# A chunk of image columns turned on GpSimd instead of ScalarE

## What is computed

```python
h = tok(x)                    # patches: einsum('bsd,hd->bsh', patches, W) + b, class token, + pos
h = concat([h, txt], axis=1)
h = h + attn(layernorm(h))    # phases tanh(x @ Wk), tanh(x @ Wq); values x @ Wv; causal sums over rows; gate; @ Wo
h = h + ffn(layernorm(h))     # 64 experts, top 2 of each row, 256 slots an expert; and a shared expert
```

## Time and profile before

| | us |
|---|---|
| median of three runs (lowest, highest) | 1647.76 (1645.76, 1649.63) |
| the profiled execution, its own time | 1646.93 |
| its span, first to last instruction | 1644.2 |
| PE busy in the span | 1455.5 |
| DVE busy | 1432.7 |
| ACT busy | 1246.3 |
| POOL busy | 1012.6 |

### The profile page before, as it was taken

One profiled execution on the slowest core, in us unless ns is written; L12 is line 12 of the kernel. 1 busy time (PEld: TensorE's weight loads), 2 busy tenths in 40 slices (PEclk: granted clock), 3 DMA queues, 4 the chain that ended last, 5 costly groups with the idle time before them and its releaser, 6 DMA issues.

```text
span 1644.2 us, 30506 instructions
## 1 busy us (share of the span) xinstructions
PE 1455.5 (89%) x9030; PEld 1121.5 (68%) x9030; DVE 1432.7 (87%) x5763; ACT 1246.3 (76%) x2190; POOL 1012.6 (62%) x857
## 2 busy tenths in 40 slices
PE   2689999999999999999999999999999972776671
PEld 1467777777777777777777777777777751555551
DVE  3369999999999999999999999999999983886661
ACT  2799999999999999999999999999999741111110
POOL 0116666666666666666666666666666665788887
PEclk9899999999999999999999999999999996998885
DMA  9977777777777777777677777777776102676653
GB/s 170 245 157 151 147 145 145 141 143 133 129 124 127 123 121 120 121 123 116 120 120 120 117 117 119 119 121 121 117 119 113 39 19 65 101 117 105 94 82 34
DMA packets 257947, 195.67 MB, mean 119 GB/s; under 512 B 59000, under 2 KB 237275, under 8 KB 257784
## 3 DMA queue, kind: packets, MB, share of 16 engines
q1 hardware_dynamic: 216280, 175.30, 59.6%
q0 software_dynamic: 39296, 17.55, 8.7%
q10 hardware_dynamic: 2208, 0.89, 0.4%
HBM read 84.28 MB, written 83.73 MB: 102 GB/s over the span
## 4 chain that ended last, share of the span: by engine, by line
PE 75%; POOL 10%; issue 5%; DVE 4%; DMA 3%; ACT 3%; SPq 1%; POOLq 0%; DVEq 0%
PE bank L896 12%; POOL out_rows L640 9%; PE bank L966 8%; PE bank L949 7%; PE bank L1037 6%; PE bank L1046 5%; PE bank L920 5%; PE bank L934 4%; PE bank L904 4%; PE bank L1053 3%; PE bank L1022 2%; PE bank L985 2%; PE bank L1012 2%; PE bank L1008 2%; PE bank L1002 2%
## 5 line engine op out<-in xcount | busy, mean ns | idle before, releaser
L596 POOL DMA_INDIRECT slot_rows<-xs,slot x640 | 648.9, 1014 | 447.4 <-DVE slot L1382 278.0
L657 ACT ACTIVATE img<-img 84x980 f32<-84x980 f32 x190 | 340.5, 1793 | 13.7 <-DMA img<-in_x 7.1
L896 PE MATMUL bank<-img,w_tok 126*128 126x392 f32 (+1 forms) x640 | 228.1, 504 | 29.2 <-DMA img<-img 23.7
L640 POOL DMA_INDIRECT out_rows<-img,etok x128 | 198.7, 1552 | 54.9 <-issue 36.1
L580 POOL TENSOR_TENSOR rs<-ve,neg_half 128x12 f32<-128x12 f32 (+1 forms) x66 | 150.0, 2273 | 111.2 <-DVE ve L1265 111.2
L896 PEld LDWEIGHTS bank<-img,w_tok 126*128 126x128 f32 (+1 forms) x640 | 124.0, 195 | 115.2 <-issue 23.9
L949 PEld LDWEIGHTS bank<-pos_a,v 128*128 128x128 f32 x768 | 139.8, 190 | 42.6
L727 ACT ACTIVATE xs<-h,nb,rs 128x128 f32<-128x128 f32 x384 | 154.1, 481 | 2.5 <-DVE nb L1271 2.5
L949 PE MATMUL bank<-pos_a,v 128*128 128x325 f32 (+2 forms) x768 | 155.7, 338 | 0.0
L740 ACT ACTIVATE xh<-h,nb,rs 128x128 f32<-128x128 f32 x384 | 154.0, 480 | 0.6 <-DVE nb L1271 0.6
L966 PE MATMUL bank<-a_t,v 128*128 128x325 f32 (+2 forms) x768 | 150.3, 345 | 0.6 <-DVE a_t L1325 0.6
(11 more groups left out here) (196 smaller groups left out, 3581.6 us busy)
## 6 DMA issues: line engine op xcount, KB each, us to landing
img<-in_x SPq DMA_DIRECT2D x384, 150.1 KB
img<-img SPq DMA_DIRECT2D x254, 160.8 KB
img<-img SPq DMA_DIRECT2D x128, 128.6 KB
out_rows<-fin SPq DMA_DIRECT2D x128, 128.0 KB
slot_rows<-xs,slot POOLq DMA_INDIRECT x640
slot_rows<-init_rows SPq DMA_DIRECT2D x16, 540.0 KB, 8.9
img<-slot_rows SPq DMA_DIRECT2D x32, 270.0 KB
h<-in_txt SPq DMA_DIRECT2D x64, 128.0 KB
```

What stands on the lines that cost most here:

```text
L596: g.indirect_dma_start(out=slots_d, out_offset=bass.IndirectOffsetOnAxis(ap=slot[0:nt, q.x, part, r:r + 1], axis=0), in_=xs[0:nt, q.x, par ...
L640: g.indirect_dma_start(out=out, out_offset=bass.IndirectOffsetOnAxis(ap=etok[:, q.load, m:m + 1], axis=0), in_=ysum[:, q.load, m, :], in_o ...
L657: a.activation(cols[:, b0:b0 + nb, :], raw[:, q.u, :].rearrange("p (t b) -> p b t", b=P)[:, b0:b0 + nb, :], ACT.Copy)\
L896: ins = mm(bank[:, 5, 0:2 * PATCHES], w_tok[r, m, :], xk[r, k.u, :, m, :], start=(m == 0), stop=(m == SHIFT - 1))
```

## The change

GpSimd turns chunk 2 of each pair from pair 2 on, at the head of its `body`, ahead of the scatters of pair k-8 and of `rstd` of pair k-4. Its waits are those that ScalarE's turn had. ScalarE leaves that chunk out, except for pair 1, and turns chunks 0 and 1 as before. The order on SP, VectorE and TensorE stays the same.

```diff
--- before.py
+++ after.py
@@ -609,9 +609,20 @@
+            def turn_columns_2(q):
+
+                wait_dma(pool, s_xin, q, 2 * C)
+                wait_dma(pool, s_spread[2], q, 2, 1)
+                b0, nb = CHUNKS[2]
+                g.tensor_copy(cols[:, b0:b0 + nb, :], raw[:, q.u, :].rearrange("p (t b) -> p b t", b=P)[:, b0:b0 + nb, :])\
+                    .then_inc(S["a_d2"], 1)
+
             def body(k):
+                p2 = k.back(2)
                 p4 = k.back(4)
                 p8 = k.back(8)
+                if p2.runs():
+                    turn_columns_2(p2)
                 if p8.runs():
                     ready(p8)
                     scatter(p8, 0)
@@ -675,7 +686,7 @@
             def early(q, n):
 
-                return (q.c, n) in ((0, 2), (0, 1), (0, 0))
+                return q.c == 0 or n == 2 and q.c > 1
```

## The result

The changed kernel takes 1673.27 us in the median (1671.41 to 1678.90), the kernel before 1647.65 beside it: a ratio of 1.0161 with a 95% interval of 1.0134 to 1.0189, so 25.6 us slower. The profiled execution after took 1672.33 us around a span of 1670.5. From L615 on (behind GpSimd's new lines), a line of the kernel before has a number higher by 11 in the changed one; each experiment's lines are those of its own trace.

The account below looks back on a forecast made before the run. TensorE was taken as the bound, VectorE 0.1 us a step behind. 57 steps x 0.6 = 34.2 us later, less 3.2 while filling, gives +31.0: 1678.8 us in the median, range 1644 to 1697.

Parts of the forecast that it names:

- TensorE bound, VectorE close behind it: Even part, 20.0 us a step: TensorE has no idle time, VectorE is 0.1 us a step behind, ScalarE has room.
- its room: VectorE in the even part: only 0.1 us a step is spent waiting for another engine.
- ScalarE's chunk: 1.55 us a pair leaves ScalarE: worth nothing in the even part, 3.2 us (0 to 4.3) while the pipeline fills.
- The copy on POOL: GpSimd's turn of chunk 2 takes 1.53 us, from 721.15 to 722.7, inside its wait for `slots`; harmless for POOL.
- a fixed 18.5 us: Landing of chunk 2's spread follows the last `slots` by 18.5 us, however long the step is.
- The wait on VectorE: Small VectorE instructions before `slots` wait 0.7 us for the copy's end; less 0.1 of room, 0.6 us a step.
- the likeliest case: The forecast wait on VectorE, at 0.45 to 0.85 us a step: 1670 to 1693 us, chance 0.58.
- The signs: Expected in the trace: step 20.5 to 20.8 us, TensorE idle 0.6 of it at L1037 or L966, ScalarE's L734 wait growing.
- No wait: Rival: the copy doesn't delay VectorE, only the 3.2 us gain is left: 1644.6 us (1643 to 1648), chance 0.22.
- A short wait: Rival: VectorE and POOL take turns, a small instruction grows 0.13 to 0.28 us: about 1650 us (1647 to 1655), chance 0.14.
- Two collisions: Rival: the copy starts right behind the scatters and `score_sum` waits too, 1.1 us: 1702 us, chance 0.06.
- The two arguments for no wait: First pair's copies ran side by side on POOL and VectorE; L1285 kept 165 ns beside `rstd`'s power: a wait of 0.

Follow-up runs that it names:

- the copy added: Kernel before, ScalarE still turning all three chunks, plus a GpSimd copy of 84x784 constant values into a tensor nobody reads: 1684.5 us, ratio 1.0221.
- the memset: Kernel before, ScalarE turning all three chunks, plus GpSimd writing 84x784 zeros and reading nothing at the changed kernel's place: 1647.62 us, ratio 1.0003.
- four values: Changed kernel, but GpSimd's copy moves only 4 values a partition instead of 784, with place and waits kept: 1644.09 us, ratio 0.9982.
- two buffers: Changed kernel with two buffers for chunk 2, its turn not waiting for the last spread: 2003.11 us, ratio 0.9832, on a chip with another bound.

## Why the prediction was right

**TensorE bound, VectorE close behind it: right; its room was mis-sized.** I took 0.1 us, from the 33 waits of `h` in the earlier trace rows. That view leaves the shortest waits out. VectorE waited for TensorE at `h` in all 57 steps, and the room there was 0.21 us; another 0.1 came back because VectorE, running earlier, meets the scatters at another point. Together 0.29.

**ScalarE's chunk: 3.2 us in the fill, nothing in the even part: right; that the traces give 3.5 is partly luck.** TensorE's wait for `xh` at pair 4 went from 2.35 to 1.08 us: 0.84 us late at the token product ahead of it, TensorE is 0.64 early behind it. The 1.56 for `sl` at pair 5 is gone, and 1.4 us with it. But two more shifts stand in the traces that I had no term for, 1 us lost before 67 us and 1.4 won between 93 and 98, and most of both goes with TensorE's granted clock. It was at half in the changed kernel from 57.0 to 60.5 us, where the kernel before had the full one, and in the kernel before from 93.8 to 97.2, where the changed one had the full one. This is the product there, before and after:

```profile
94.65 3.58 PE L966 MATMUL bank<-a_t,v 128*128 128x325 f32 x12
```

```profile
92.99 0.79 PE L1033 MATMUL bank<-const,xh 128*128 128x128 f32 x6 [1.08 <-ACT xh L751]
93.62 2.32 PE L977 MATMUL bank<-a_t,v 128*128 128x325 f32 x12
```

So one pair of traces can't give this term to a microsecond. More of them can tell its sign: pair 5's product starts at 132.5 to 134.0 us in the three traces in which ScalarE turns chunk 2 (before, the copy added, the memset), and at 125.5 to 129.0 in the six with it on GpSimd on chips like these. The medians of the two versions with a step of 20.0 us give 3.2 (four values) and 2.5 us (1.3 to 4.3; `v_hb`).

**The copy on POOL: right in the mean.** 1544 ns in the median where I had 1530, in POOL's wait; VectorE waited for POOL's `rs` in only three steps, 1.4 us in all. Taken over the steps of the trace (starts of L617 and L1387, ends of L1393) it starts 0.55 us before L1387 in the mean and 18.7 us behind the last `slots`, where I had 0.77 and 18.5. So counting packets gave the mean to 0.2 us, but "a fixed 18.5 us" was wrong: it is 16.7 to 20.1.

**The wait on VectorE: right in kind and place, and two terms were off in opposite directions, which is luck.** The victim is L1387, not only L1388, so the wait begins 0.09 us earlier, and with each copy's place it varies from nothing to the whole of the copy (172 to 1547 ns). The loss is 0.78 in the mean against my 0.7. Net of 0.29 of room it is 0.5 instead of 0.6, times 58 steps 28.4 instead of 34.2. That is the term that makes 1673.3 out of 1678.8. With the right room and my own 0.7 the sum would have been 57 x 0.41 = 23.4, less 3.2: 1668, below the 1670 to 1693 of the likeliest case.

**The signs.** TensorE's idle time is 0.4 us a step where I had 0.6; it stands at L1048 (L1037 before), as forecast, but more of it at L953, which waits for `cum`, and not at L966. ScalarE's wait at L734 grew as forecast, from 50.7 to 60.8 us.

**The rivals.** No wait: refuted by L1387's 801 ns. A short wait of at most 0.28: L1387's is longer in the mean. Two collisions: `score_sum` was not met in the changed kernel; with two buffers it was, as that rival described. The two arguments for no wait still stand as facts. The first pair's copies on POOL and VectorE ran side by side: what waits here is a tensor_scalar or has two operands in SBUF, and that copy is neither. And L1285, which has two, begins 1.1 us into POOL's power of 2.3 us and doesn't wait for it. I don't know why; no run varied the power.

The Trainium skill (SBUF — State Buffer, Who interferes with whom) has the pair of ports as an exclusive lock that whoever starts first keeps for the whole instruction, and has two-operand instructions contend only with a GpSimd instruction that reads. The copy started by `value_rows` (2205 ns, `residual` 949) and the memset agree. The two runs with the copy right behind a scatter agree only if "starts" is not the recorded start. L1285 beside the power (165 ns) doesn't agree.

## A version that beats both

The turn on GpSimd that waits for `v_hb`, two scatters, `rstd`, eight scatters: 1644.86 us, 0.17% below the kernel before (0.9974 to 0.9992) and 1.7% below the changed one. Its even part equals the one before (1288.3 - 127.5 = 1160.8 us), and its fill is shorter. At 0.17% it keeps what leaves ScalarE, as the run with four values did, and no more. On the two chips with the other bound the same kernel was 0.4% slower and 0.6% faster than the kernel before, so this holds for chips like the first.

## What to carry to other kernels

Busy time moved to an idle GpSimd is free only if VectorE, in that stretch of the step, runs nothing of the two kinds that were seen to wait here: no instruction with two operands in SBUF and no tensor_scalar over SBUF. Read VectorE's timeline under the new instruction's place before choosing it, and start it by a semaphore of VectorE's own rather than by a landing that drifts. A wait for the last victim ahead of a free stretch costs nothing when POOL has slack. And a copy directly behind an indirect DMA needs some 0.7 us more of free space ahead of it. When you size the room of the engine that is second, measure from one fixed instruction to the others over many steps: a list of waits can leave out short ones that come in every step.

## What the hardware showed that I had not expected

- A copy queued right behind an indirect DMA keeps out VectorE's instructions that begin up to some 0.6 us before it (0.16 us became 2.16, 0.94 became 2.97). From 0.66 us on `residual` passes, and the copy takes 0.1 us longer; L1435 was still kept out at 0.64 to 0.66. Whether the DMA instruction doesn't give the port back or the copy takes it early is open.
- An indirect DMA by itself (0.97 us on POOL) stops a tensor_scalar only in its second half: one that begins up to 0.51 us into it passes (161 to 165 ns), one that begins from 0.53 us on ends with it (up to 443 ns). `residual`, with two operands in SBUF, isn't stopped.
- Between copies queued on GpSimd one waiting instruction of VectorE gets in each time (pieces of 0.51 us).
- A memset of 0.75 us stops a tensor_scalar (0.17 us became up to 0.84) but, in the two steps that can tell, not instructions with two operands in SBUF.
- Two of the chips ran the same unchanged kernel in 2035 to 2043 us, with ScalarE waiting some 5 us a step; the traces don't show for what.
